# A transformer layer on one Trainium2 core: next group's rows loaded earlier, and the value matmuls in runs

## The reference

```python
x = _layernorm(tgt, ln1_g, ln1_b)
q, k, v = (_heads(t) for t in jnp.split(x @ sa_wqkv, 3, axis=-1))
wei = softmax(where(causal & ~padding, einsum('bhtd,bhsd->bhts', q, k) * scale, -inf))
result = tgt + _merge(einsum('bhts,bhsd->bhtd', wei, v)) @ sa_wproj + sa_bproj
xq, xs = _layernorm(result, ln2_g, ln2_b), _layernorm(src, ln2_g, ln2_b)
k2, v2 = (_heads(t) for t in jnp.split(xs @ ed_wkv, 2, axis=-1))
q2 = _heads(xq @ ed_wq)
wei2 = softmax(einsum('bhtd,bhjd->bhtj', q2, k2) * scale)
result = result + _merge(einsum('bhtj,bhjd->bhtd', wei2, v2)) @ ed_wproj + ed_bproj
h = relu(_layernorm(tgt, ln3_g, ln3_b) @ ff_w1 + ff_b1)
return result + h @ ff_w2 + ff_b2
```

## Time and profile before

| | us |
|---|---|
| median of 3 runs | 676.9 |
| lowest, highest | 673.03, 678.33 |
| the profiled execution | 671.41 |
| its span on the core | 669.5 |

### The profile page before, as it was taken

How to read it: one execution, slowest core, us unless ns; L and a number is a source line. 1 busy time by engine, 2 the same in 40 slices (tenths; PEclk the granted TensorE clock), 3 DMA queues, 4 the chain that set the end, 5 groups by cost and what they waited for, 6 DMA issues and landing times.

```text
span 669.5 us, 14170 instructions
## 1 busy us (share of the span) xinstructions
PE 590.5 (88%) x5564; PEld 447.6 (67%) x5564; DVE 415.0 (62%) x982; ACT 326.9 (49%) x613; POOL 128.6 (19%) x370
## 2 busy tenths in 40 slices
PE   3497797699999998699999998899999999999696
PEld 3385576576777776576777776676777777767564
DVE  5984563678557644678557644678557644685371
ACT  2133453336635655346635655346635655365064
POOL 6701310203003210203003211103003211130010
PEclk9966998799999999799999999699999999999798
DMA  8294049176560049176570048176570057005700
GB/s 234 75 132 85 1 86 143 41 93 74 107 126 24 10 92 141 43 96 73 107 125 23 12 95 143 36 96 75 109 125 19 11 93 129 24 2 103 92 2 15
DMA packets 73122, 52.08 MB, mean 78 GB/s; under 512 B 21920, under 2 KB 72288, under 8 KB 73056
## 3 DMA queue, kind: packets, MB, share of 16 engines
q1 hardware_dynamic: 73056, 51.17, 46.0%
HBM read 14.36 MB, written 1.84 MB: 24 GB/s over the span
## 4 chain that ended last, share of the span: by engine, by line
PE 49%; DVE 15%; SPq 13%; DMA 10%; ACT 7%; issue 3%; POOL 2%; DVEq 0%; POOLq 0%; ACTq 0%
SPq L532 12%; PE misc L1068 9%; DMA tb<-in_x 6%; PE pvb L1039 6%; PE scb L1023 6%; PE mxb L1007 5%; PE misc L925 5%; DVE negm L837 5%; PE misc L927 4%; PE misc L926 4%; PE misc L1075 4%; DMA k2st<-kp 2%; DVE rem L771 2%; ACT prob L708 2%; PE misc L1046 1%
## 5 line engine op out<-in xcount | busy, mean ns | idle before, releaser
L708 ACT ACTIVATE prob<-scb 125x448 f32<-125x448 f32 (+1 forms) x256 | 137.5, 543 | 74.3 <-PE scb L1023 68.7
L837 DVE TENSOR_REDUCE negm<-mxb 112x1 f32<-112x375 f32 x256 | 130.4, 540 | 25.2 <-PE mxb L1007 23.4
L1039 PE MATMUL pvb<-prob,v 125*17 125x112 f32 (+1 forms) x2048 | 96.4, 266 | 0.3 <-ACT ot L715 0.3
L1007 PE MATMUL mxb<-k2st,q2st 96*112 96x375 bf16 x256 | 87.1, 356 | 2.4 <-DVE negm L837 1.6
L1023 PE MATMUL scb<-q2st,k2st 128*125 128x112 bf16 x768 | 78.5, 225 | 0.2
L1023 PEld LDWEIGHTS scb<-q2st,k2st 128*125 128x125 bf16 x768 | 66.3, 137 | 16.9 <-issue 8.8
L627 POOL CAST mparts<-negm 112x8 bf16<-112x8 f32 x64 | 12.2, 191 | 333.4 <-DVE negm L837 175.4
L834 DVE TENSOR_REDUCE negm<-mxb 112x4 f32<-112x448 f32 x64 | 39.6, 619 | 43.8 <-PE mxb L1004 43.6
L1068 PE MATMUL misc<-wf,hT 128*112 128x256 f32 x256 | 60.9, 386 | 3.2 <-DVE rem L771 3.2
L1039 PEld LDWEIGHTS pvb<-prob,v 125*17 125x17 f32 (+1 forms) x2048 | 35.0, 95 | 35.8 <-issue 21.7
L1068 PEld LDWEIGHTS misc<-wf,hT 128*112 128x112 f32 x256 | 44.9, 179 | 14.6 <-DVE rem L771 4.8
(11 more groups left out here) (153 smaller groups left out, 1238.2 us busy)
## 6 DMA issues: line engine op xcount, KB each, us to landing
k2st<-kp SPq DMA_DIRECT2D x192, 93.8 KB, 4.3
xs<-in_ctx SPq DMA_DIRECT2D x16, 375.0 KB
q1st<-qp SPq DMA_DIRECT2D x48, 112.0 KB, 5.6
k1st<-kp SPq DMA_DIRECT2D x48, 112.0 KB, 7.0
q2st<-qp SPq DMA_DIRECT2D x96, 56.0 KB, 2.3
xn<-in_x SPq DMA_DIRECT2D x4, 448.0 KB, 12.2
tb<-in_x SPq DMA_DIRECT2D x8, 224.0 KB, 10.0
out<-ostage SPq DMA_DIRECT2D x16, 112.0 KB, 3.3
```

The costliest lines, as they stand in the source:

```text
L708: nc.scalar.activation(prob[0:rows, n % PROB_SLOTS, :], scb[n % SCORE_BANKS][0:rows, 0:GH * T], ACT.Exp, scale=SCALE).then_inc(s_ex, 1)
L837: V.tensor_reduce(negm[:, at, i:i + 1], mx[0:T, 0:S], axis=AX_X, op=ALU.max, negate=True).then_inc(s_mx, 1)
L1007: mm = M(mx[0:T, 0:S], q2st[0:NROW, i, b * T:(b + 1) * T], k2st[k2_place(q, b)][0:NROW, i, 0:S], start=True, stop=True)
L1039: mm = M(pvb[32 * j:32 * j + VW, g * T:(g + 1) * T], vals, prob[0:rows, slot, j * T:(j + 1) * T], start=(c == 0), stop=(c == chunks(u) - 1))
```

## The change

- `load_tgt` moves from quarter (2, 0) of its period to quarter (6, 0) of the period before. The first group's load stands at the very start of the list, as it did.
- `resid` of the sequences 2 and 3 moves from (2, 1) to the end of the parts of (3, 0), behind `stats1` and `norm1`.
- The `pv` steps of a quarter no longer alternate with scores. In a cross unit the three chunks of a quarter stand in one run behind the first score of the next quarter. In a self unit the `pv` of all four quarters stand in one run behind the first score of the next unit.
- `PROB_SLOTS` becomes 6.

```diff
-PROB_SLOTS = 5
+PROB_SLOTS = 6
...
-        (2, 0): [("load_tgt",), ("load_tb", 1), [("sT", 1, 0), ("sT", 1, 1)]],
-        (2, 1): [("ff1", 4), ("k2", 1, 0), ("stack_k2", 1, 0), ("resid", 1), ("k2", 1, 1), ("stack_k2", 1, 1)],
+        (2, 0): [("load_tb", 1), [("sT", 1, 0), ("sT", 1, 1)]],
+        (2, 1): [("ff1", 4), ("k2", 1, 0), ("stack_k2", 1, 0), ("k2", 1, 1), ("stack_k2", 1, 1)],
...
-        (3, 0): [("norm1",), ("ff1", 7), ("load_src", 3)],
+        (3, 0): [("norm1",), ("ff1", 7), ("load_src", 3), ("resid", 1)],
...
-        (6, 0): [("ff1", 1), ("norm2", 0)],
+        (6, 0): [("load_tgt",), ("ff1", 1), ("norm2", 0)],
...
+    def weighted_with(u, g):
+
+        if u >= BG:
+            run = [("pv", u, g, c) for c in range(chunks(u))]
+        else:
+            run = [("pv", u, h, 0) for h in range(4)] if g == 3 else []
+        return run + ([("ot", u)] if g == 3 else [])
+
...
             own = [[("score", u, g, c)] for c in range(chunks(u))]
-            if n:
-                v, h = quarters[n - 1]
-                weighted = [[("pv", v, h, c)] for c in range(chunks(v))]
-                weighted[-1] += [("ot", v)] if h == 3 else []
-                own = [part for pair in zip_longest(own, weighted) for part in pair if part]
+            if n and weighted_with(*quarters[n - 1]):
+                own.insert(1, weighted_with(*quarters[n - 1]))
...
-    placed = [(t[0], R if t in head else R - 1) + t[1:] for R in range(groups + 1) for t in steps]
+
+    placed = [("load_tgt", 0)] + [(t[0], R + 1 if t[0] == "load_tgt" else R if t in head else R - 1) + t[1:]
+                                  for R in range(groups + 1) for t in steps]
```

More of the change, by code:

```diff
@@ L27 @@
 from contextlib import ExitStack
-from itertools import zip_longest
 import concourse.bass as bass
```

## The result

The changed kernel takes 645.4 us (median of 4 runs, 644.9 to 650.1) against 675.9 us (median of 4, 673.0 to 678.3) for the kernel before: the ratio on record is 0.961, with a 95% interval of 0.957 to 0.965. The forecast was 643, in a range from 627 to 662. The profiled execution after took 644.9 us with a span of 643.0; before it was 671.4 with 669.5. So the spans differ by 26.5 us.

A forecast was written before the change was run, and what follows sets the result against it. PE's own order was taken as the path nearly everywhere, with stops at period starts and costly narrow-form changes. A 20 plus B 13 made 33 us off 676.9, giving 643.9, stated as 643; range 627 to 662 (8 in 10).

The forecast's parts named there:

- A: Period starts: moving `load_tgt` and `resid` removes `mT` waits on POOL (12.6 us) and slow clock (7.5): 20 us, bounds 3.6 to 21.4.
- B: PE: `pv` steps in runs save 0.265 us a join; 13 us after losses off the path, bounds -7 to 38.
- stack chain: From (5, 1) to (0, 1): SP's 24 stack DMAs, 20.5 us to the split, don't shrink; 2.0 us of PE's saving lost.
- Where DVE is full: Units 4 and 6: DVE nearly always busy, so PE's savings of 1.6 and 1.1 us a group are lost there.
- `v2` behind the split: `v2` 3 comes behind the `k2` split's wait in the new order; its six matmuls cost 0.85 us a group.
- The bank waits: Scores wait for exponentials with two banks, at starts of units 5 and 7 and in units 4 and 6: 1.0 us a group.
- rival 4: Slower, chance 0.03: bank waits in each of the 64 cross quarters stop PE up to 1.10 us, 689 us.
- `ff2`: The 1.06 us wait ahead of `ff2` should go, since `mT` now comes ahead of `qk1`.
- (1): B is nothing, chance 0.12: SP's stack chain, DVE and the banks take all of PE's saving; 657 us.
- (2): B counts nearly in full, chance 0.10: struck-out savings return as a chain waiting less starts the next sooner; 625 us.
- (3): A changes nothing, chance 0.05: `resid` still holds POOL, or PE waits for `norm1` or `xT`; 664 us.

The follow-up runs named there:

- A alone: Kernel before with only the changed places of `load_tgt` and `resid`, `pv` steps and five slots as before: 656.0 us, ratio 0.974.
- v2_first: Changed kernel with `v2` 3 0 joined to `stack_k2` 3 1, so that it stands ahead of `mT` again: 645.4 us, ratio 0.958.
- k2_tgt_62_v2: Changed kernel with `k2` 2 stacks ahead of `q2`, `load_tgt` in (6, 2), and `v2` 3 0 ahead of `mT`: 638.0 us, ratio 0.948.
- B alone: Changed kernel with the moves of `load_tgt` and `resid` undone, leaving the `pv` runs and six slots: 668.9 us, ratio 0.991.
- tgt_joined: Changed kernel with `load_tgt` and `ff1` 1 tied as one part of (6, 0): 644.2 us, ratio 0.957.
- slots5: Changed kernel with five `prob` slots instead of six: 645.0 us, ratio 0.957.
- k2 first: Changed kernel with both `k2` 2 and their stacks ahead of both `q2` in (5, 1): 643.5 us, ratio 0.956.
- k2_tgt_62: Changed kernel with `k2` 2 stacks ahead of `q2` in (5, 1) and `load_tgt` in (6, 2): 639.6 us, ratio 0.951.

## Why the prediction was right, and where not

**The sum.** The working forecast a span of 636.5, and it was 643.0: of 33 us came 26.5. The medians moved by 30.5 because the profiled execution of before was 4.5 us under its median. The time of 645.4 lies 2.4 us over the forecast. Some of that closeness is luck: the forecast started from a median of 676.9, while the kernel before had 671.3 to 674.5 in the three later batches, and 33 us below those would be 638 to 641.5. By the ratio the saving is 26 of the 33.

**A, predicted 20 us; alone 14.5 between the spans' last marks, 17.7 by the ratio.** The mechanism stood. In A alone, in the second and third period, all three of its signs are there: no `mT` wait over 1 us for POOL at the start, no `xn` wait on DVE, clock 1.00. In the changed kernel the first sign fails as it was written, by a tenth (1.09 to 1.10 us in each start), but at another `mT` and by B; see below. A alone gave 18.5 us in the six stages of the three starts (4.19 + 1.18 + 5.42 + 1.16 + 3.60 + 2.93). The prologue, which varies by that much between traces, shows 1.4 more, and the other stages lost 5.4. For this, and for the 1.5 us that the starts lie below 20, the working lacked these things:

- "I let nothing take the place of that wait" held for the second and third start. In the first there is another stop some 15 us ahead, in the changed kernel 4.10 us of `mT` at 106.33, for a split of which ACT's part waited 4.56 us for the landing of `k2st`; the clock falls there whatever A does. It stood in the trace before, 3.10 us at 107.64; I had taken only the waits for POOL. The first start gave 5.4 us in A alone: the wait of 4.0, and 1.4 of the 5.11/2 that I counted for the clock.
- `load_tgt` costs nothing on SP in its new place, but it takes a turn there and pushes `ff1` 1 behind a `pv` on PE: 0.84 us in each of three periods, 2.5 in all. I had looked at SP's and POOL's order for this step, not at PE's. In the last period A alone loses 1.15 us, for which I have no cause. And in the first period A alone loses 2.19 us in (1, 0), at the stops of 0.89 and 0.66 us at the stack chain, with the clock down to 0.50 behind them.
- The load doesn't go where I read the idle DMA engines. I took their share of 0.01 at 360 to 365 for the new place, but in A alone SP issued it at 340.55, some 9 us before PE came to that quarter's `ff1` (349.39) and 0.47 us behind `tb`, where their share was 0.61 and then 0.99 (windows 340:342 and 342:344). It was in time all the same: DVE's `stats`, some 60 us later, doesn't wait.

**B, predicted 13 us; 11.4 on top of A by the marks (25.86 - 14.51), 8.4 by the ratios.** The working had 3.8 us in each of the first three periods and 1.8 in the last; the marks give 5.9, 2.9, 2.1 and 0.4. In the first, 1.9 of the 5.9 are what A alone lost more in (1, 0). The others are low by stages with a slow clock: (2, 0), (3, 0) and (3, 3). So that 13 and 11.4 lie close is in part errors that cancel. PE's busy time fell by 30.8 us (30 or more was the sign). A run of 24 takes 0.77 us and the next matmul starts 0.70 after it; one of 32 takes 0.96, the next starts 0.89 after: 0.19 for each further step, as taken from the earlier trace rows.

```profile
113.72 0.96 PE L1045 MATMUL pvb<-prob,v 112*17 112x112 f32 x32
114.61 0.37 PE L1013 MATMUL mxb<-k2st,q2st 96*112 96x375 bf16 x1
...
167.98 0.77 PE L1045 MATMUL pvb<-prob,v 125*17 125x112 f32 x24
168.68 0.39 PE L931 MATMUL misc<-wv_hi,xsT_hi 128*125 128x256 f32 x1
```

- *Where DVE is full*: unit 4 gave 0.27 us of six joins' 1.6, unit 6 lost 0.40, unit 7 gave 1.54 to 1.61. That was the split into path and no path that the forecast rests on, and DVE is full there after the change too (busy for 4.00 of 4 us in 289:293, in the second period's unit 4). The Trainium skill says in "TensorEngine Tiling (Array Packing)", PSUM Bottleneck, that after a speedup of TensorE by tiling the emptying of PSUM may become the bottleneck. Here TensorE got faster by fewer changes of form and not by more tiles; with that, units 4 and 6 agree with the page (0.27 us gained and 0.40 lost), and unit 7 doesn't (1.54 to 1.61 gained).
- *The stack chain*: it is fixed, as I said, 20.0 us against 20.5. But the growth of its wait was mis-sized. I took 2.0 us of PE's saving as lost there and gave "3 us or more" as the sign; ACT's wait grew from 1.15, 1.34 and 1.72 to 1.56, 1.62 and 2.57 us, and in the last period from 5.5 to 6.27. PE's work from the first stack to the point at which the split waits was 19.2 us (337.14 - 1.34 - 316.64) and is 18.4 (318.46 - 1.62 - 298.43): it shrank by 0.8, not 2.0. Unit 5 kept 1.1 us of what I struck out.
- *`v2` behind the split*, 0.85 a period: right in place, wrong in kind. The stages that it ends lose 0.26, 1.52 and 2.41 us, and what goes with that is the clock, which my sum counted at the period starts only: 0.57 behind the stop of 1.60, 0.50 behind that of 2.55, 1.00 behind that of 1.53. By `v2_first` (second period) and `k2_tgt_62_v2` such a stage costs nothing, or gives 0.5 to 0.9 us, when the stops are shorter or parted.
- *A wait that was not in the working*: one `mT` of the third quarter waits for POOL's splitting, 1.10, 1.10, 1.09 and 1.52 us in the four periods (122.79, 263.08, 404.47, 545.19). Before and in A alone only the last of the four waits, 0.54 and 0.53 us; B alone has it too, 1.05 us at 128.96. The maximum that POOL needs comes late from DVE (POOL starts at 261.93, having waited 5.47 us for it), and it isn't `resid`, which was done at 256.5. So this belongs to B and its order: 4.3 us in all, of which I had none. Behind the last of these waits the clock fell. It stands here in PE's timeline, then the windows from there on:

```profile
545.19 0.21 PE L1057 MATMUL misc<-identb,mparts 112*24 112x112 bf16 x1 [1.52 <-POOL mparts L639]
...
545.00:547.00 2.00, 1.81 (x6) 1.49 (x7) 1.00 (x2) 0.91 (x1) 0.05 (x1) 0.64 0.28 96
547.00:549.00 2.00, 2.00 (x6) 1.42 (x5) 0.00 (x0) 0.00 (x0) 0.00 (x0) 0.51 0.00 1
```

  The stage that this falls in, (3, 3), loses 1.96 us. In `tgt_joined` the same wait of 1.52 us left the clock at 1.00 (windows 547:551), and the stage loses 0.28. So 1.7 us went with the fall.
- *The bank waits*, 1.0 us a group: scores wait for exponentials for 4.2 us in all, 0.4 at the longest. This was right, and with it rival 4, which needed 0.9 us a quarter, is out. The six slots play no part in it: `slots5` takes the same time.
- *`ff2`*: its wait went from 1.06 to 0.35 us, not to nothing.

**The rivals.** B was not nothing (1): 645.4 against 657, and A alone is 8.4 us slower than both by the ratios. It was not full (2), 625: the chain, the clock behind it, and DVE kept most of it. A was not nothing (3): 645.4 against 664, and A alone gives 17.7 us.

## What to carry to other kernels

Ask of every wait on an in-order engine what stands ahead of the waiting instruction in its queue, and of every load what stands ahead of it in the queue that issues it: here a load issued eight quarters sooner, some 50 us, was worth 14 us, and `resid`, which waits for the load behind it, moved alone, 4. A saving on the busiest engine counts only in stages where nothing fixed ends them; price it stage by stage, with marks that repeat in both traces, and expect that a chain freed (k2 first) shows the next one a few microseconds behind it. A step's place in a list is not its time (a queue that waits for nothing between two places issues at the same moment from either), but its turn counts on every engine, also on those that have nothing in it. And wherever an edit adds a stop of 1 to 2 us on PE, read the granted clock behind it: here up to 3.3 us a stage went with it.

## What the runs showed of the hardware

- SP issued six stack DMAs in 3.75 us (298.43), 0.62 us each, and another six in 5.04 us (310.69). The chain of 24 took 16.5 us to issue before (316.64 to 333.11) and 17.3 after (298.43 to 315.73); 24 at 0.62 would be 15 us, an estimate.
- The rows of `tb` for two sequences (224 KB), for which POOL waited each time, were used between 2.8 us (changed kernel, issued at 476.00) and 8.0 us (`k2_tgt_62`, issued at 194.09) after their issue.
- The clock fell after stops much shorter than the 3 to 5 us of the period starts: one of 1.60 us (319.80) was followed by 0.57 and 0.58, and two of 0.89 and 0.66 close together by 0.50, while one of 1.53 (ended at 179.43) and a pair of 0.97 and 0.66 left it at 1.00. The same wait of 1.52 us had 0.51 behind it in the changed kernel (545.19) and 1.00 in `tgt_joined` (547.41), and of the stops of 1.03 and 1.02 us in (3, 0) only the second, in `k2_tgt_62`, had 0.50 behind it. The stop of 4.1 us at 106.33 has 0.60 about it. From these runs I can't say what besides its length makes a stop count.
